# Graph network on one core: score and message slots laid out in one stage, pick matmuls in bf16 with numbers in two exact parts

## What is computed

```python
h = jnp.maximum(_layernorm(x, axis=-1), 0.0)
x = x + _L0_gnn_ref(h, edge_index, gate_w, gate_b)          # gated, softmax over dst
h = jnp.maximum(_layernorm(x, axis=-1), 0.0)
x = x + _L1_gnn_ref(h, edge_index, Wl, bl, Wr, br, att, ...) # two GATv2 layers, 4 heads
h = jnp.maximum(_layernorm(x, axis=-1), 0.0)
x = x + _L2_gnn_ref(h, edge_index, deg)                      # mean over incoming edges
h = jnp.maximum(_layernorm(x, axis=-1), 0.0)
x = x + _L3_gnn_ref(h, src, dst, W_self1, W_neigh1, ...)     # two SAGE layers
```

## Time and profile before

| | us |
|---|---|
| runs, median of 3 | 3445.32 (3443.18 to 3447.86) |
| the profiled execution, time | 3452.38 |
| its span, first to last instruction | 3450.4 |
| mean granted TensorE clock | 0.912 of full |
| TensorE / VectorE / ScalarE / GpSimd busy | 2609.4 / 2286.9 / 1001.6 / 817.2 |

### The profile page before, as it was taken

How to read it: one execution, slowest core, us unless ns; L and a number is a source line. 1 busy time by engine, 2 the same in 40 slices (tenths; PEclk the granted TensorE clock), 3 DMA queues, 4 the chain that set the end, 5 groups by cost and what they waited for, 6 DMA issues and landing times. The chain is left out here.

```text
span 3450.4 us, 53250 instructions
## 1 busy us (share of the span) xinstructions
PE 2609.4 (76%) x12797; PEld 1556.3 (45%) x12797; DVE 2286.9 (66%) x10981; ACT 1001.6 (29%) x2296; POOL 817.2 (24%) x858
## 2 busy tenths in 40 slices
PE   3775695287888888379857788888855995698998
PEld 1443583144444444246643444444433665244444
DVE  4666664577888888954497688888895447333323
ACT  0776692050000000135525000000012553233333
POOL 0000000016666666200000666666630000000000
PEclk8999797589999999689988899999977998898999
DMA  0000600038888888255423888888834552500000
GB/s 23 2 1 3 252 1 14 24 131 275 283 284 284 283 280 283 64 127 149 134 45 114 272 286 283 280 285 278 283 108 98 152 149 57 236 1 7 16 17 19
DMA packets 396226, 507.40 MB, mean 147 GB/s; under 512 B 29059, under 2 KB 331908, under 8 KB 394532
## 3 DMA queue, kind: packets, MB, share of 16 engines
q0 software_dynamic: 66560, 274.39, 23.6%
q1 hardware_dynamic: 329380, 229.61, 23.0%
HBM read 409.28 MB, written 94.61 MB: 146 GB/s over the span
## 5 line engine op out<-in xcount | busy, mean ns | idle before, releaser
L914 POOL DMA_INDIRECT rows<-row_table,idx x832 | 792.1, 952 | 797.5 <-POOLq L132 324.2
L965 PE MATMUL z_ps<-xr,hot_ta 128*128 x2496 | 693.4, 387 | 212.5 <-DVE rows L1008 183.1
L976 PE MATMUL z_ps<-rows,ident 128*128 128x256 f32 x1664 | 573.9, 427 | 5.0 <-issue 3.5
L2069 PE MATMUL dense_ps<-cnt,h 128*128 128x512 f32 (+1 forms) x1050 | 417.3, 555 | 86.9 <-ACT cnt L2027 83.3
L965 PEld LDWEIGHTS z_ps<-xr,hot_ta 128*128 128x128 bf16 x2496 | 243.8, 98 | 512.3 <-issue 396.9
L1008 DVE SCALAR_TENSOR_TENSOR rows<-rows,att_all 128x128 f32<-128x128 f32 x1664 | 423.4, 290 | 37.1 <-remote 23.6
L1034 DVE TENSOR_TENSOR rows<-z_ps,rows 128x256 f32<-128x256 f32 x832 | 348.2, 418 | 109.7 <-PE z_ps L976 73.0
L1008 DVE SCALAR_TENSOR_TENSOR rows<-z_ps,att_all 128x128 f32<-128x128 f32 x1664 | 410.2, 281 | 12.8 <-issue 12.5
L1343 PE MATMUL acc_m<-xr,hot_m 128*128 x1984 | 342.1, 295 | 69.6 <-issue 29.8
L1343 PEld LDWEIGHTS acc_m<-xr,hot_m 128*128 128x128 f32 x1984 | 270.9, 193 | 184.2 <-issue 181.1
L2069 PEld LDWEIGHTS dense_ps<-cnt,h 128*128 128x128 f32 x1050 | 189.6, 193 | 295.4 <-issue 198.5
(11 more groups left out here) (399 smaller groups left out, 3226.4 us busy)
## 6 DMA issues: line engine op xcount, KB each, us to landing
xr<-kept_rows SPq DMA_DIRECT2D x124, 512.0 KB
kept_rows<-rows SPq DMA_DIRECT2D x416, 128.0 KB
spread_a<-rel_rows SPq DMA_DIRECT2D x208, 128.0 KB
counts_line<-counts SPq DMA_DIRECT2D x1, 19550.0 KB
counts<-counts_line SPq DMA_DIRECT2D x6, 3200.0 KB
rows<-row_table,idx POOLq DMA_INDIRECT x832
row_table<-xl_ring SPq DMA_DIRECT2D x50, 258.0 KB
rows<-row_table SPq DMA_DIRECT2D x32, 320.0 KB
```

Of the source, the lines that this page charges most:

```text
L914: nc.gpsimd.indirect_dma_start(out=rows[:, u, :], out_offset=None, in_=table, in_offset=bass.IndirectOffsetOnAxis(ap=c.idx[:, n:n + 1], ax ...
L965: nc.tensor.matmul(ps[:, n % Z, :], hot, tile[:, m, 0:HC], start=m == 0, stop=False, skip_group_check=True)
L976: nc.tensor.matmul(ps[:, n % Z, HALF_C:HC], c.ident[:, :], rows[:, n % ROWS, HALF_C:HC], start=False, stop=True, skip_group_check=True).th ...
L2069: last = nc.tensor.matmul(ps[:, SUM, q % 2, 0:size * W_NODES], h[:, k, :], cnt[:, n % BUFS, 0:size * W_NODES], start=k == 0, stop=k == NOD ...
```

## The change

`message_slots` is gone; its steps stand in `make_slots`, in one stage with the score slots. Each chain has its own semaphores, and the two are interleaved by hand on VectorE: score counting, message counting, the split of the edge numbers into parts, score picks, message picks, score results, message results, the rows for the trip to DRAM, the message table, then the breaks. `dst` is loaded once, on SyncE's queue; `src` is loaded on ScalarE's queue. The pads of `dst` take one value that serves both lists.

All pick matmuls, also those of `window_slots`, take bf16 operands. `pick` holds 0 and 1 and is written as bf16. A number that bf16 doesn't hold exactly is split into its bf16 rounding and the rest, and the two are summed in PSUM; `lo`, `hi` and the ones need one part. The widened copies are gone: the stationary operand repeats one column by its access pattern (`to_broadcast`). The four copies of `any_break` for each side are one. `c.slot_first` is gone, so the tables allocated behind it lie 32 bytes lower.

```diff
-        dst_f = sb("dst_f", [P, EDGE_BLOCKS, P])
-        src_f = sb("src_f", [P, EDGE_BLOCKS, P])
+        both_f = sb("both_f", [P, 2, EDGE_BLOCKS, P])
+        both_1 = sb("both_1", [P, 2, EDGE_BLOCKS, P], BF16)
+        both_2 = sb("both_2", [P, 2, EDGE_BLOCKS, P], BF16)
...
+            @block.scalar
+            def _(act):
+                act.wait_ge(s["pads"], 2)
+                edges(act, src, src_i, s["src_in"])
+                act.wait_ge(s["src_in"], 3 * 16)
...
+                sp.wait_ge(s["pads"], 1)
+                edges(sp, dst, dst_i, s["dst_in"])
...
+                dve.wait_ge(s["ends_in"], EDGE_BLOCKS * 16)
+                m_link(nc.vector.tensor_copy(ends_i[:, 1, :], dst_i[:, :, P - 1]))
...
+                dve.wait_ge(s["src_in"], 3 * 16)
+                link(nc.vector.tensor_copy(both_f[:, :, :, :], both_i[:, :, :, :]))
+                link(nc.vector.tensor_copy(both_1[:, :, :, :], both_f[:, :, :, :]))
+                nc.vector.tensor_tensor(out=both_2[:, :, :, :], in0=both_f[:, :, :, :], in1=both_1[:, :, :, :],
+                                        op=ALU.subtract).then_inc(s["parts"], 1)
...
-                    nc.vector.tensor_scalar(shift_w[:, b, :], c.ones[:, :], shift[:, b:b + 1], None, ALU.mult)
-                    link(nc.vector.tensor_scalar(from_first[:, b, :], slot_no[:, :], first[:, b:b + 1], None, ALU.is_ge))
-                    link(nc.vector.scalar_tensor_tensor(out=pick[:, b, :], in0=slot_no[:, :], scalar=end[:, b:b + 1],
-                                                        in1=from_first[:, b, :], op0=ALU.is_lt, op1=ALU.mult))
...
+                    link(nc.vector.tensor_scalar(from_first[:, b, :], slot_no[:, 0:SLOTS], first[:, b:b + 1], None,
+                                                 ALU.is_ge))
+                    nc.vector.scalar_tensor_tensor(out=pick[:, b, :], in0=slot_no[:, 0:SLOTS], scalar=end[:, b:b + 1],
+                                                   in1=from_first[:, b, :], op0=ALU.is_lt, op1=ALU.mult)\
+                      .then_inc(s["picked"], 1)
...
-                    for h in range(H):
-                        link(nc.vector.tensor_copy(any_break[:, k, :, h], through[:, :, edge]))
+                    nc.vector.tensor_copy(any_break[:, k, :, :],
+                                          through[:, :, edge:edge + 1].to_broadcast([SB, SLOT_BLOCKS, H]))\
+                      .then_inc(s["broken"], 1)
...
+                pe.wait_ge(s["parts"], 1)
+                pe.wait_ge(s["picked"], EDGE_BLOCKS)
+                spread(SRC, SLOTS, (lambda b: both_1[:, 1, b, :], lambda b: both_2[:, 1, b, :]))
+                spread(DST, SLOTS, (lambda b: both_1[:, 0, b, :], lambda b: both_2[:, 0, b, :]))
+                spread(TIL, SLOTS, (lambda b: wide(starts_1[:, 1, b:b + 1]), lambda b: wide(starts_2[:, 1, b:b + 1])))
+                spread(USE, SLOTS, (lambda b: ones_b[:, :],)).then_inc(s["slots"], 1)
+                pe.wait_ge(s["m_picked"], EDGE_BLOCKS)
+                spread(M_DST, MSLOTS, (lambda b: both_1[:, 0, b, :], lambda b: both_2[:, 0, b, :]))
+                spread(M_WIN, MSLOTS, (lambda b: wide(m_shift_1[:, b:b + 1]), lambda b: wide(m_shift_2[:, b:b + 1])))
...
                 nc.vector.tensor_copy(dst_f[:, :, :], dst_i[:, :, :])
+                link(nc.vector.tensor_copy(dst_1[:, :, :], dst_i[:, :, :]))
...
+                nc.vector.tensor_tensor(out=dst_2[:, :, :], in0=dst_f[:, :, :], in1=dst_1[:, :, :], op=ALU.subtract)
...
+                for half in range(2):
+                    spread(WIN, half, (lambda b: shift_1[:, b:b + 1].to_broadcast([P, P]),
+                                       lambda b: shift_2[:, b:b + 1].to_broadcast([P, P])))
+                    spread(DST, half, (lambda b: dst_1[:, b, :], lambda b: dst_2[:, b, :]))
+                    spread(LO, half, (lambda b: lo_b[:, b, :],))
+                    last = spread(HI, half, (lambda b: hi_b[:, b, :],))
...
-        message_slots(nc, c, dst)
```

More of the change, by code:

```diff
@@ new lines, in wide, with edges @@
+        def wide(col):
+            return col.to_broadcast([P, P])
+        with phase(nc, pads=0, dst_in=0, src_in=0, ends_in=0, iotas=0, vec=0, m_vec=0, counted=0, m_counted=0, parts=0,
+                   before=0, m_before=0, picked=0, m_picked=0, slots=0, m_slots=0, rel=0, turned=0, broken=0, breaks=0,
+                   m_win=0, m_turned=0, row_parts=0, rows_out=0, rows_back=0) as (block, s):
+            whole = EDGES_FULL // P * P
+            def edges(queue, ap, to, sem):
+                queue.dma_start(to[:, 0:whole // P, :],
+                                ap[0:whole * P].rearrange("(b p e) -> p b e", p=P, e=P)).then_inc(sem, 16)
+                queue.dma_start(to[0:EDGES_FULL - whole, whole // P, :],
+                                ap[whole * P:EDGES_FULL * P].rearrange("(p e) -> p e", e=P)).then_inc(sem, 16)
+                queue.dma_start(to[EDGES_FULL - whole:EDGES_FULL - whole + 1, whole // P, 0:EDGES_REST],
+                                ap[EDGES_FULL * P:E].rearrange("(a e) -> a e", a=1)).then_inc(sem, 16)
@@ L314, in _ @@
-                last.then_inc(s["pe"], 1)
-                pe.wait_ge(s["vec"], V + 2 * (2 + SLOT_BLOCKS + H + 1))
-                for k, at in ((0, BRK), (1, PRE)):
+                for sem, bank, n, before, done in (("counted", BEFORE, n_slots, n_before, "before"),
+                                                   ("m_counted", M_BEFORE, m_slots, m_before, "m_before")):
+                    pe.wait_ge(s[sem], EDGE_BLOCKS - 1)
+                    to = ps[:, bank, 0:EDGE_BLOCKS]
+                    nc.tensor.matmul(to, later[:, :], n[:, :], start=True, stop=False)
+                    nc.tensor.matmul(to, c.ones[:, :], before[:, :], start=False, stop=True).then_inc(s[done], 1)
@@ new lines, in spread @@
+                def spread(bank, n, parts):
+                    for b in range(EDGE_BLOCKS):
+                        for k, left in enumerate(parts):
+                            last = nc.tensor.matmul(ps[:, bank, 0:n], left(b), (pick if n == SLOTS else m_pick)[:, b, :],
+                                                    start=b == 0 and k == 0,
+                                                    stop=b == EDGE_BLOCKS - 1 and k == len(parts) - 1)
+                    return last
+                pe.wait_ge(s["parts"], 1)
@@ L521, in norm_relu @@
+                    last.then_inc(s["breaks"], 1)
 def norm_relu(nc, c, x, out, gain=None, shift=None, dot=None):
@@ L2256, in graph_layers @@
         c.slot_tile = sb("slot_tile", [1, SLOTS], I32, within=early)
-        c.slot_first = sb("slot_first", [P, 2, EDGE_BLOCKS], within=early)
         c.m_rel = sb("m_rel", [P, MSLOTS], within=early)
```

467 lines of the change are left out of this document (209 added, 258 removed).

## The result

| | before | after |
|---|---|---|
| median of the runs, us | 3446.59 (3443.18 to 3450.76) | 3386.12 (3385.03 to 3387.15) |
| ratio, 95% interval | | 0.9824 (0.9807 to 0.9841) |
| profiled execution, time / span | 3452.38 / 3450.4 | 3386.57 / 3384.8 |
| mean granted TensorE clock | 0.912 | 0.92 |

The change saves 60.5 us in the medians. The forecast was 3380.0 with a range of 3370 to 3397, so the time lies inside, 6.1 us above the point. Of these, 1.3 are not the change's: the forecast subtracts from a median of 3445.32 for the kernel before, which has 3446.59 here.

The account below looks back on a forecast made before the run. No engine was busy in the three slot stages, chains waiting between VectorE, TensorE and DMA queues. Window stage -12.5 and merged stage -52.7 make -65.2 us, from the median 3445.3 to 3380.0 us, range 3370 to 3397.

Parts of the forecast that it names:

- the sum of stages: Whole kernel: barriers keep stages from overlapping, so stage differences add up, -12.5 - 52.7 = -65.2 us.
- the merged chain: Score and message slots as one interleaved stage: 56.3 us in place of 109.0, so -52.7 us.
- the message table would cover the trip to DRAM: Merged stage: the 15.85 us message table chain hides the rows' 9.05 us trip, with 6.8 us to spare.
- the window stage: Window slots: 48 bf16 matmuls take 9.9 us, 13.1 less; VectorE work ahead grows 0.6; net -12.5 us.
- By that rule the cost is nothing: Score stages' gathers: a 32-byte table shift only permutes row starts that already take every 16-byte place; cost zero.
- Rival 3: Score stages' gathers slowed by the 32-byte layout shift: mild 3393 to 3405 us, chance 0.05; full 3482, chance 0.02.
- the stages here depend on nothing that varies between runs, so I subtract from the median: Touched stages: the 65.2 us saving is taken from the median of the runs, 3445.3, giving 3380.1 us.
- a sign of being wrong: Score stages: a change in their length of over 3 us would show the prediction wrong.
- Rival 1: Window and merged stages: TensorE stays at 1.2 GHz through all picks, +5.9 and +9.3 us, 3395; chance 0.07.
- Rival 2: Pick matmuls miss the bf16 price, 0.30 us each, through repeated column or two-part accumulation: 3393 us; chance 0.06.
- Rival 4: Merged stage: VectorE waits in program order, so late loads hold both chains; 5 us gives 3385, within the forecast.
- The pick without a wait: Merged stage: a pick without a wait saves some 0.12 us, eight times; by the skill's rule, 1.0 us longer in sum.

Follow-up runs that it names:

- the kernel before once more: The kernel before, unchanged, run and profiled again on a faster chip: 3255.75 us, ratio 1.000 (0.999 to 1.001).
- the merged stage with float32 picks: Against the kernel before, only the merging and interleaving; picks stay float32, window stage as before: 3220.23 us, ratio 0.9893.
- the second profile of the change: The changed kernel, unchanged, run again beside the one with 32 bytes put back: 3194.19 us, ratio 0.9807 against the kernel before.

## Why the prediction was right, and where it missed

**Right: the sum of stages.** Reading each stage between its barriers and adding the differences gave -65.2; the stages that the change touches show -64.2 (-11.3 and -52.9), the kernel before once more and the change on the two faster chips -65.8 (-12.4 and -53.4).

**Right: the merged chain, nearly step by step.** Forecast 56.3 us from first memset to last copy, measured 56.0. Dst landed at 3.5 (3.2), the ends' wait was 0.64 (none or a few tenths), score picks started at 15.7 (14.9), tile_f was reached at 22.1 (21.9), waits at m_win, rel_row and brk_before were none, as forecast. The wait at tile_f was 0.98 where 1.5 was expected: VectorE and the picks' start both came 0.8 later, and the picks then took 6.5 us to tile_f in place of 7.0. That the message table would cover the trip to DRAM is confirmed.

**Mis-sized: the window stage**, -11.5 against -12.5. The slow part of the picks lasted until about 40.3, some 5 us, where I took 3.8 from the float32 burst of the earlier trace rows. The work ahead of the picks grew by 0.8 us, not 0.6. That makes 10.6 us where the term said 9.9, and 0.8 where it said 0.6. The 9.9 itself lies inside what the same code shows in other executions (9.6 to 10.7), and the float32 picks took 22.96 to 24.34 us in four; so most of this miss is how long the slow part happened to last.

**Failed: "By that rule the cost is nothing", and no term for the shift in the sum.** Rival 3 had the right cause at the wrong place and in the wrong size. I weighed the shift of 32 bytes only for the score stages' gathers, whose rows are 2576 bytes apart, and these indeed did not change (626.3 us in the kernel before and 627.3 in the change on the faster chips). I did not look for tables whose rows all start at the same place against 128 bytes. The own rows do, with 512 bytes from one to the next, and they cost 4 to 5 us. The Trainium skill ("DMA: Bandwidth & Descriptors", section "How a descriptor splits into AXI transactions") says that a descriptor which doesn't start at a 256-byte boundary costs more, since the bytes between the boundary below and its start are fetched too. The trace agrees that place matters, but not on the unit: of two places 128 bytes apart at most one is a multiple of 256, and both were fast (210 and 217 GB/s). The runs show 128. The prediction's "a further transaction" also said more than that section does: by its count, an estimate, a row of 2576 bytes takes eleven transactions from any start at a multiple of 16.

**Failed: "the stages here depend on nothing that varies between runs, so I subtract from the median".** The subtraction was fair, but the sentence let me read the profile's difference as exact. The score stages differed by 4.5 us together between the first two profiles and by about 1 each between others, with nothing in the code to cause it. The second of them moved by 3.3 us, beyond the 3 us that the prediction named as a sign of being wrong; the sign was set inside the scatter, and the repeats, not that row, cleared the mechanism.

**The rivals.** Rival 1 (half clock through all picks): refuted, eight picks start 0.166 us apart from 41.79. Rival 2 (no bf16 price with a repeated column): refuted by the same rows, `w_shift`, whose operand is one column repeated, and `w_dst`, whose isn't, both take 1.49 us for eight. Rival 3: 5 us in place of 13 to 102. Rival 4 (waits in program order): 0.6 us at the tile ends and nothing more. Rival 1 is refuted for the whole burst only: about half of the window burst, 5 of 10.6 us, did run at the half clock.

**The pick without a wait.** The row at 555.54 is 0.65 us long and the next starts 0.57 after it; before, with a wait behind the pick, the next started 0.69 after it (562.07 to 562.76). So the price by the row held in the changed kernel too. The Trainium skill ("VectorE: DVE Perf Modes", section "The DRAIN you can't avoid") has the semaphore at no extra cost, measured on eight copies, and adds that a next instruction which is not held starts earlier. These rows fit the second case: the wait costs 0.12 us.

## What to carry to other kernels

Where stages end in a barrier and no engine is busy, write down each chain with its waits and lay another chain's independent work into them; the gain is bounded by the waits, and the last engine's own work is the floor (48 of 56 us here). Cheaper matmuls and an interleave shorten the same waits: write each wait down before you add the two gains. Here they added up (12.7 and 16.7 us), and the waits were then used up; more of either could have gained at most the 1 us of waiting that was left.
A dropped or added small tensor moves everything that is allocated behind it: list the start of each DMA destination before and after, and check first those whose rows all start at one place against 128 bytes. The 32 bytes of padding cost no time here and gave back 5 us.

## What the runs showed of the hardware

- The same stage ran at different speeds on different chips: the score stages took 624 to 628 us on two chips, 721 to 724 and 732 to 737 on two others. At the same DMA share of 0.88 the table by stretch of before shows 281 GB/s in the middle of it and on one of the faster chips:

```profile
689.78:1316.11 626.33, 585.80 (x2668) 318.91 (x2722) 606.04 (x4326) 93.47 (x361) 396.66 (x416) 0.98 0.88 299
```

All stages without gathers agreed within about 2 us. What differs between the chips stays open.
- How long TensorE stays at the half clock differs between executions of the same code. In the profile after, the count stage behind the window picks starts at half clock, after 20.72 us without work, and goes on so until about 77.6, though TensorE works almost without a break from 71.6 on:

```profile
66.66 3.57 PE L1818 MATMUL count_ps<-zeros 128*128 128x512 bf16 x8 [20.72 <-PEq L132]
77.28 0.54 PE L1832 MATMUL count_ps<-h 128*128 128x200 bf16 x2
77.88 0.34 PE L1832 MATMUL count_ps<-h 128*128 128x200 bf16 x2
```

  This does not come from the bf16 picks: the run with float32 picks in the window stage (the merged stage with float32 picks) shows it as long, and the second profile of the change shows only the first eight matmuls slow. It costs nothing that can be seen: from the first matmul of the count stage to the first VectorE instruction of the next stage, all fourteen profiles take 253.3 to 254.0 us. In the window stage, where VectorE waits for TensorE, float32 matmuls ahead of the burst removed the slow part.
- 512-byte rows written 32 bytes below or 64 bytes above the old place ran at 185 GB/s over 11 us, in place of 210 at the old place and 217 at one 128 bytes above.
